# First chunk of a fused state space, retention and expert layer: B and C spread by matmuls, constants on three queues, weights centred earlier, own places for the end chunks

## What is computed

```python
x = _layernorm(x + mamba(x, ...))            # state space part, 256 channels, 16 states
x = _layernorm(x + retention(x, ctx, ...))   # 64 x 64 scores per sequence, decay mask
x = _layernorm(x + experts(x, ...))          # 16 experts, top 2, and a shared one

# mamba
x_b, z = jnp.split(x @ W_in, 2, axis=-1)
xc = _silu(conv_b + sum(xpad[:, k:k + T, :] * conv_w[:, k] for k in range(4)))
proj = xc @ W_xproj                          # 8 + 16 + 16 columns
delta_raw, B_in, C_in = ...                  # the three parts of proj
delta = jax.nn.softplus(delta_raw @ W_dt + b_dt)
A_bar = jnp.exp(delta[..., None] * -jnp.exp(A_log))
Bx = delta[..., None] * B_in[:, :, None, :] * xc[..., None]
# h = A_bar * h + Bx along the tokens; y = sum over states of h * C_in, + D_param * xc
out = (y * _silu(z)) @ W_out
```

## Time and profile before

| what | value |
|---|---|
| median of 3 runs | 1140.01 us (1138.7 to 1140.21) |
| the profiled execution | 1139.9 us, of which its span is 1138.0 us |
| mean granted clock of TensorE | 0.976 |
| DVE busy | 1047.7 us (92%) |
| PE, ACT, POOL busy | 1036.2, 992.5, 991.4 us |
| first drive starts | 30.17 us |
| last scan starts | 1062.91 us |

### The profile page before, as it was taken

One profiled execution on the slowest core, in us unless ns is written; L12 is line 12 of the kernel. 1 busy time (PEld: TensorE's weight loads), 2 busy tenths in 40 slices (PEclk: granted clock), 3 DMA queues, 4 the chain that ended last, 5 costly groups with the idle time before them and its releaser, 6 DMA issues. The chain is left out here.

```text
span 1138.0 us, 18240 instructions
## 1 busy us (share of the span) xinstructions
PE 1036.2 (91%) x5831; PEld 738.1 (65%) x5831; DVE 1047.7 (92%) x1458; ACT 992.5 (87%) x2159; POOL 991.4 (87%) x608
## 2 busy tenths in 40 slices
PE   5686888999999999999999999999999999989997
PEld 3464666676766766676676767667676767666665
DVE  2999999999999999999999999999999999999521
ACT  5878799999999999998989999899999999898442
POOL 0577798999989898998989899898989999899854
PEclk9778899999999999999999999999999999999999
DMA  6544454555546464555646455564736556453221
GB/s 159 204 162 159 160 176 162 179 191 180 189 167 200 166 196 177 186 179 177 206 148 218 148 187 182 177 201 156 228 136 213 193 178 194 169 185 116 84 94 52
DMA packets 84111, 194.49 MB, mean 171 GB/s; under 512 B 17288, under 2 KB 47936, under 8 KB 67632
## 3 DMA queue, kind: packets, MB, share of 16 engines
q1 hardware_dynamic: 84016, 193.33, 51.0%
HBM read 179.14 MB, written 5.77 MB: 162 GB/s over the span
## 5 line engine op out<-in xcount | busy, mean ns | idle before, releaser
L937 POOL TENSOR_TENSOR read<-state,bc_all 128x1024 f32<-128x1024 f32 x256 | 605.2, 2368 | 53.7 <-DVE state L811 43.9
L811 DVE TENSOR_TENSOR_SCAN state<-decay,drive_bank 128x512 f32<-128x512 f32 (+1 forms) x464 | 594.4, 1316 | 3.6 <-POOL read L937 1.9
L761 ACT ACTIVATE decay<-delta,a_neg 128x252 f32<-128x252 f32 x1024 | 422.5, 495 | 0.9
L803 DVE TENSOR_TENSOR drive_bank<-dx_bank,bc_all 128x512 f32<-128x512 f32 (+1 forms) x496 | 330.1, 702 | 0.3 <-DMA bc_all<-bc_dram 0.2
L373 PEld LDWEIGHTS y_bank<-ident,read 128*128 128x128 f32 x2048 | 241.0, 145 | 87.3 <-POOL read L937 46.4
L373 PE MATMUL y_bank<-ident,read 128*128 128x128 f32 x2048 | 277.4, 280 | 21.2 <-POOL read L937 20.9
L982 POOL TENSOR_TENSOR hid<-gu,comb_all 128x512 f32<-128x512 f32 (+1 forms) x136 | 165.3, 1216 | 21.3 <-DVE gu L897 12.4
L364 PEld LDWEIGHTS down_bank<-down_w,hid 128*128 128x128 f32 x1024 | 127.1, 192 | 30.7 <-issue 27.5
L731 ACT ACTIVATE silu<-bank 128x512 f32<-128x512 f32 (+1 forms) x153 | 87.6, 575 | 58.9 <-PE bank L364 58.2
L364 PE MATMUL down_bank<-down_w,hid 128*128 128x128 f32 x1024 | 136.0, 277 | 1.5 <-POOL hid L982 1.5
L364 PE MATMUL bank<-x2T,up_w 128*128 128x512 f32 (+1 forms) x272 | 132.1, 570 | 0.7 <-ACT silu L731 0.7
(11 more groups left out here) (127 smaller groups left out, 1358.7 us busy)
## 6 DMA issues: line engine op xcount, KB each, us to landing
bc_all<-bc_dram SPq DMA_DIRECT2D x128, 1024.0 KB, 4.9
comb_all<-comb_dram SPq DMA_DIRECT2D x240, 128.0 KB, 4.8
x_in<-in_x_dram SPq DMA_DIRECT2D x15, 256.0 KB, 5.3
ctx_in<-in_ctx_dram SPq DMA_DIRECT2D x15, 256.0 KB, 5.3
k_pair<-k_pair SPq DMA_DIRECT2D x30, 128.0 KB, 2.4
q_pair<-q_pair SPq DMA_DIRECT2D x30, 128.0 KB, 2.1
out_dram<-y_out SPq DMA_DIRECT2D x15, 256.0 KB, 6.1
comb_all<-comb_dram SPq DMA_DIRECT2D x32, 64.0 KB, 2.6
```

Of the source, the lines that this page charges most:

```text
L761: done = e.activation(seqs(decay_t[j % DECAYS][:, i, h, :])[:, :, 1:T], seqs(delta[c % 2][:, h, sub * SUB:(sub + 1) * SUB])[:, :, 1:T], AC ...
L803: e.tensor_tensor(drive_bank[:, a:b, :, :], dx_bank[:, :, :].unsqueeze(1).to_broadcast(shape), bc_all[group % BC_BUFS][:, 0, PAIR * i + a: ...
L811: e.tensor_tensor_scan(states(state_t[j % STATE_BUFS], a, b), states(decay_t[j % DECAYS], a, b), states(drive_bank, a, b), 0.0, ALU.mult, ...
L937: e.tensor_tensor(read_t[j % READS][:, :, :, :], state_t[j % STATE_BUFS][:, :, :, :], bc_all[group % BC_BUFS][:, 1, PAIR * i:PAIR * (i + 1 ...
```

## The change

1. **B and C of the first group by matmul.** For chunk 0 PE multiplies a column of the identity, spread over 128 output columns, with the 40 rows of `proj`; each product is one row of `proj` on all 128 partitions. Eight of them (256 columns each) fill `down_bank` and `y_bank`, two at a time, as scratch; DVE copies them to `bc_all` in four instructions (128x512). Groups 1 and on of chunk 0 still go through `bc_dram`.
2. **Chunk 0's short path.** DVE, not ACT, copies `proj`; DVE writes `dx_bank` directly, with neither POOL's `dx` nor ACT's copy. `d_diag` moves to just before the first drive. `w_dt` is loaded and used with 8 rows, not padded to 40 with zeros.
3. **Constants on three queues.** ACT issues `ident`, `a_log`, `conv_w`, and the two of `conv_b`; POOL issues `w_out` and `down_w` behind its memsets; SP the rest, where `qkv_rows`, `router_rows`, `shared_rows` come at tick -15, and the others at ticks -7 and 1, behind the store of chunk 0's B and C. The shared semaphores are split by what they cover.
4. **Tables.** ACT runs a one-column activation with Exp at the start, with Silu after the first `xT` and with Softplus after the first `xc`, so that the table of each is loaded there. `a_neg` is made by ACT at the start.
5. **Centring.** `w_out` and `down_w` are centred right after chunk 0's third tap, before the copy of `proj`; `w_qkv` and `shared_w` after the fourth scan. Chunk 1's three taps move behind the first drive and scan.
6. **Places.** `AT` gets five columns (all chunks, last, last but one, first, second). The last but one is the old common column. The common one differs from the old in some places, by up to 15 ticks.

```diff
+COLUMN = [3, 4] + [0] * (CHUNKS - 4) + [2, 1]
...
-    "y_gated": [(41, 56), (69, -24)],
+    "y_gated": [(40, 56, 41, -2, 38), (69, -24, 69, 36, 68)],
...
-    "comb_load": [(136, 134), (143, 149), (144, 156), (150, 169), (154, 181), (157, 190), (159, 212), (166, 235)],
+    "comb_load": [
+        (140, 134, 140, 102, 136), (143, 149, 143, 112, 137), (147, 156, 144, 119, 140), (151, 169, 150, 127, 142),
+        (152, 181, 154, 137, 162), (154, 190, 157, 138, 163), (169, 212, 159, 146, 166), (174, 235, 169, 151, 167)],
...
# PE
-                        mm(bank.t[:, 0:width(c)], w_dt[:, h * P:(h + 1) * P], proj[:, 0:width(c)]).then_inc(S["dt_mm"], 1)
+                        mm(bank.t[:, 0:width(c)], w_dt[:, h * P:(h + 1) * P], proj[0:DT_RANK, 0:width(c)]).then_inc(S["dt_mm"], 1)
                         bank.free = (S["delta"], at(c, h, 2))
+                    if c == 0:
+                        for two in (0, 1):
+                            for pair in (0, 1):
+                                w.wait_ge(S["bc_copy"], 2 * two + pair - 1)
+                                for i in range(PAIR):
+                                    row = DT_RANK + GROUP * pair + PAIR * two + i
+                                    done = mm((down_bank, y_flat)[pair][:, i * SUB:(i + 1) * SUB],
+                                              ident[0:PROJ, row:row + 1].to_broadcast([PROJ, P]), proj[0:PROJ, 0:SUB])
+                                done.then_inc(S["bc_mm"], 1)
...
# ACT
+            def warm(i, func):
+
+                e.activation(warmed[:, i:i + 1], eps_col[:, 0:1], func, scale=1.0)
...
+            e.dma_start(ident[:, :], io["c_ident"]).then_inc(S["ident"], 16)
+            e.dma_start(a_log[:, :, :], io["L0_attn_A_log"].rearrange("(h p) n -> p h n", p=P)).then_inc(S["a_log"], 16)
+            e.dma_start(conv_w[:, :, :], io["L0_attn_conv_w"].rearrange("(h p) k -> p h k", p=P)).then_inc(S["conv_consts"], 16)
+            per_channel(e, conv_b, io["L0_attn_conv_b"], S["conv_consts"])
+            w.wait_ge(S["zero"], DECAYS + 2)
+            warm(0, ACT.Exp)
+            w.wait_ge(S["a_log"], 16)
+            e.activation(a_exp[:, :, :], a_log[:, :, :], ACT.Exp, scale=1.0).then_inc(S["a_exp"], 1)
+            w.wait_ge(S["a_exp"], 1)
+            e.activation(a_neg[:, :, :], a_exp[:, :, :], ACT.Copy, scale=-1.0).then_inc(S["a_neg"], 1)
...
# DVE
+            def bc_copy(two, pair):
+
+                w.wait_ge(S["bc_mm"], 2 * two + pair + 1)
+                e.tensor_scalar(bc_all[0][:, pair, PAIR * two:PAIR * (two + 1), :].rearrange("p n t -> p (n t)"),
+                                (down_bank[:, :], y_flat)[pair], 1.0, 1.0, ALU.mult, ALU.mult).then_inc(S["bc_copy"], 1)
...
+                    w.wait_ge(S["proj_mm"], 1)
+                    e.tensor_scalar(proj[:, 0:SUB], bank_of["proj", 0][0:PROJ, 0:SUB], 1.0, 1.0, ALU.mult, ALU.mult).then_inc(
+                        S["proj"], 1)
...
+                    bc_copy(0, 0)
+                    w.wait_ge(S["delta"], 2)
+                    w.wait_ge(S["xc"], HALVES)
+                    e.tensor_tensor(dx_bank[:, :, :], xc[0][:, :, 0:SUB], delta[0][:, :, 0:SUB],
+                                    ALU.mult).then_inc(S["first_dx"], 1)
+                    bc_copy(0, 1)
+                    bc_copy(1, 0)
+                    bc_copy(1, 1)
+                    w.wait_ge(S["d_consts"], 16 * 2)
...
-                        (0, -3, ((w_out[:, :, :], 0, HALVES), (down_w[:, :, :], HALVES, PAIRS))),
-                        (1, 5, ((w_qkv[:, 2:3, :], HALVES + PAIRS, 1), (shared_w[:, 2:3, :], HALVES + PAIRS + 1, 1)))):
+                        (0, CENTER_TICK, ((w_out[:, :, :], 0, HALVES), (down_w[:, :, :], HALVES, PAIRS))),
+                        (1, 15, ((w_qkv[:, 2:3, :], HALVES + PAIRS, 1), (shared_w[:, 2:3, :], HALVES + PAIRS + 1, 1)))):
...
# POOL
+            e.dma_start(w_out[:, :, :], io["L0_attn_W_out"].rearrange("(h p) n -> p h n", p=P)).then_inc(S["out_consts"], 16)
+            e.dma_start(down_w[:, :, :], io["L0_ffn_down_proj"].rearrange("k e d -> (k e) d").rearrange(
+                "(j p) d -> p j d", p=P)).then_inc(S["out_consts"], 16)
```

More of the change, by code:

```diff
@@ L289, in blocks_of, with loads @@
             return width(c) // P
+        def loads(buffer, groups):
+            return uses(groups, buffer, BC_BUFS) - (1 if buffer == 0 else 0)
         def uses(before, buffer, buffers):
@@ L788, in _ @@
                     for h in range(HALVES):
-                        e.tensor_scalar(d_diag[:, h, :], ident[:, :], d_param[:, h:h + 1], 1.0, ALU.mult, ALU.mult)
-                    w.wait_ge(S["a_exp"], 1)
-                    e.tensor_scalar(a_neg[:, :, :], a_exp[:, :, :], -1.0, 1.0, ALU.mult, ALU.mult).then_inc(
-                        S["mamba_dve"], 1)
+                        done = e.tensor_scalar(d_diag[:, h, :], ident[:, :], d_param[:, h:h + 1], 1.0, ALU.mult, ALU.mult)
+                    done.then_inc(S["d_diag"], 1)
@@ L1029, in _ @@
-            e.dma_start(gate_w[:, :, :], io["L0_ffn_gate_proj"].rearrange("k d e -> d k e")).then_inc(late, 16)
-            e.dma_start(up_w[:, :, :], io["L0_ffn_up_proj"].rearrange("k d e -> d k e")).then_inc(late, 16)
-            for i in range(2):
-                e.dma_start(ctx_t[i][:, 0:blocks_of(i), :], rows_of(io["ctx_1024"], i)).then_inc(S[f"ctx_load{i}"], 16)
-            for tick in range(FIRST_TICK, LAST_TICK):
+            e.dma_start(w_dt[:, :], io["L0_attn_W_dt"]).then_inc(early, 16)
```

313 lines of the change are left out of this document (170 added, 143 removed), and 5 rows, old and new, of the table EXP_AT.

## The result

The changed kernel took 1144.65 us in the median of 9 runs (1140.29 to 1151.66), the kernel before 1140.01; the ratio is 1.0048, with a 95% interval of 1.0024 to 1.0071. It is 0.5% slower, where 0.7% faster was forecast. A second set of 12 runs of the same code gave 1.0051 (1.0031 to 1.0072). Two things stand out beside the median: the spread of its runs is 11 us, that of nine runs of the kernel before under 4; and the profiled execution, 1140.29 us with a span of 1138.5, is the fastest of the nine. What it shows is the loss of a good execution.

A forecast was written before the change was run, and what follows sets the result against it. DVE, with hardly a gap, was taken to bound the body of 256 steps, between a head and a tail chain. 1139.9 - 5.8 (head) - 2.4 (body waits) - 0.3 (tail) = 1131.4, said as 1131.5; range 1127.5 to 1137.0 us.

The forecast's parts named there:

- The head: Start until the first drive: from 30.17 to 22.3 us, less 2.1 for chunk 1's taps, a gain of 5.8 us.
- The 3.0 us taken for the landing of the tap rows: Head: SP's third transfer, issued by 1.7, lands in 3.0 us; `w_tap` is done by 5.8, no obstacle.
- a rise inside the new matmuls: Head, PE: TensorE's clock rises during the new matmuls, between 4.1 and 7.1 us for them; first drive at 22.3.
- Rival B: Head: `w_out` and `down_w` come late on POOL's queue and delay the copy of `proj`; landing at 13: 1135. Chance 0.08.
- Rival D: Head: something else sets the first drive, ACT's start or late B and C groups; 2 us left, 1138. Chance 0.08.
- Rival A: Head, PE: clock stays low through all new matmuls; first drive 24.3, head gain 3.8, 1133.4 us. Chance 0.18.
- The taps: Chunk 1's three taps, 2.27 us of DVE, move from before the first drive into the body; 2.1 us taken.
- DVE's busy time was to rise by 3 to 4 us: Sign of being right: DVE's busy time rises by the copies, 3 to 4 us, all in the head.
- The passage on the queues: Head: by the skill's rule, spreading constants over queues is worth only the issues' time, 0.50 us each, 2.5 us.
- `w_qkv`'s centring stays in the body either way: Head sum: this centring is in the body before and after the change, so it was given no cost.
- They can take away only waits: Body: the changed common places remove only DVE waits, 2.4 us of 5.3 taken off, bounds 0 and 5.3.
- Rival C: Body, common chunks: DVE's scans wait for POOL's `read`; with 1.0 us in each of 13, 1144.5. Chance 0.10.

The follow-up runs named there:

- again: The changed kernel run once more, for a second trace, against the kernel before: 1144.59 us, ratio 1.0051.
- part_c15: Changed kernel with only the retention and expert operations of chunks 0 and 1 at the old kernel's places: 1137.22 us, ratio 0.9984 to the kernel before.
- c01_part: Changed kernel, `w_qkv` and `shared_w` centred after the fourth step's drives, chunks 0 and 1's retention and expert operations at old places: 1134.89 us, 0.9953 to the kernel before.
- c1_common: Changed kernel, `w_qkv` and `shared_w` centred after the fourth step's drives, chunk 1's retention and expert operations at common places: 1151.47 us, 1.0091 to the kernel before.
- headfill: Changed kernel, `w_qkv` and `shared_w` centred after the fourth step's drives, seven matmuls of zeros in PE's idle time before 12 us: 1141.82 us, 1.0011 to the kernel before.

## Why the prediction was wrong

**Right, in part by luck.** The head came out near its forecast times: `xT` ended at 5.35 (5.5 forecast), `w_xproj` ran 12.43 to 13.49 (11.0 to 12.9 forecast), the centring 10.46 to 13.80, the first decays began at 17.13, ahead of the drive, and the first drive at 21.45 and 22.24 (22.3). The 3.0 us taken for the landing of the tap rows were 5.3 in fact, and the quicker matmuls made up for it. That was luck, and so was the time of the new matmuls: I had `w_xproj` and `w_dt` at the lower level and a rise inside the new matmuls. In the traces of the changed kernel and of `again` TensorE is at its upper level from `w_xproj` on and falls inside them (from 1.02 us for four recorded ones to 2.07 and 1.91), and no trace here has the rise. Rival B was not seen: `row_sum` never waited for POOL's transfers. Rival D neither. Rival A is real, in some executions, worth 4 us in the head. The taps cost 1.9 us against 2.1.

DVE's busy time was to rise by 3 to 4 us and rose by 8.5 (1047.7 to 1056.2): 3.6 are the copies, `dx_bank` and `proj`, 2.7 the centring below, 1.5 the 32 multiplies by the gate, whose move the forecast had at nothing. The passage on the queues put item 3 at the time of its issues, 2.5 us for the five that ACT has. It did not weigh that the store of B and C had stood 5.1 us in SP's queue (17.00 to 22.14) and no longer would.

**Wrong, first step: "`w_qkv`'s centring stays in the body either way".** I costed a moved step at nothing since its work is the same. Its work is; its neighbours are not. Beside a `read` that has just begun this instruction waits for nearly all of it. That term was 0 and is 2.7 us in the trace, 3 to 3.5 in the time. A row that could have told is in DVE's timeline of before; POOL's `read` stands below it:

```profile
35.77 0.40 DVE L841 TENSOR_SCALAR row_mean<-row_sum 128x2 f32<-128x2 f32 x1
33.78 2.37 POOL L937 TENSOR_TENSOR read<-state,bc_all 128x1024 f32<-128x1024 f32 x1 [12.82 <-DVE state L811]
```

The same operation on ten columns took 0.17. It ended at 36.17, POOL's `read` at 36.15; I took no notice of 0.2 us.

**Wrong, second step: "They can take away only waits".** I weighed the new common places and took 2.4 us off. Measured alone they move the median by nothing that can be measured (0.9997, 0.9988 to 1.0006), though the gaps in their trace fell from 5.40 to 2.54. The places of chunks 0 and 1, which the forecast didn't cost at all, were another matter. Those of their retention and expert operations were the loss, 7.5 us in the time (in the traces 5 us of gaps, 9.08 against 4.11 in `part_c15`). As I read it, this is the ramp, where the expert part of chunk 0 meets the retention of chunk 1 and the lists of three engines are new to each other; no run shows that this meeting is the cause. Rival C had the right kind of mechanism, but I put it into the common chunks, on POOL, and the waits were in the first four, mostly on PE and ACT.

The forecast's sum with the terms as measured: 1139.9 - 8.7 + 1.9 + 2.7 (centring) + 3.7 (gaps) + 1.3 (drives and scans, a term that I didn't have) = 1140.8 at the 128th scan; 0.7 us more came up to the last scan, and the tail was 1.1 us shorter, so 1140.4, where the profiled execution took 1140.3. The median is 4 us above that. What makes the spread is open. The level of TensorE in the head can be a part (4 us between the first drives of traces of the same start), but with the head filled the spread was still 8 us. It is 3 us in six runs with the places and the centring undone, so waits in the ramp may multiply it; that is not shown. No execution of 1151 us of the changed kernel was caught by the profiler.

Open: which of the 47 operations of the retention and expert part is the badly placed one. `c01_part` moves them together. That `c1_common` made it 8 us worse shows only that chunks 0 and 1 have to be placed with each other.

## What to carry to other kernels

Where the bound engine has hardly a gap behind its start, a quicker start is worth about as much at the end (a delay of 4 us put in by hand came out as 3.5; in `c01_part` the first drive is 8.1 us sooner, 1.9 go for the taps, and 5.3 come out), but only if the order behind it still fits: where a hand-written order is changed in many places at once, give each group of places its own run. Read the small instructions of the bound engine for length, not only its gaps: two of them held 2.7 us that no list of waits names. And before a trip through memory is replaced by matmuls, look for what its store waits for: of the thirteen microseconds from `proj` to the first drive here, five were a place in a queue.

## What the runs showed of the hardware

A DVE instruction can be held while a GpSimd instruction runs, and its recorded length grows by the wait: `row_mean` of two columns took 0.17 us with POOL idle, and 0.40, 0.86 and 2.05 us beside POOL's `read`, each time ending within 0.05 us of it. In `c01_part` a router instruction of 128x32 did the same beside POOL's `k_pair` (120.14 to 122.48); in the kernel before the same instruction took 0.19 us:

```profile
121.09 1.45 DVE L952 TENSOR_TENSOR above<-logits,top 128x32 f32<-128x32 f32 x1
122.46 0.15 DVE L954 TENSOR_TENSOR lead<-top 128x2 f32<-128x2 f32 x1
```

Others were not held beside a `read`: `row_sum` (0.27), and the drives and scans, which have an operand in PSUM (0.69 and 1.21). The Trainium skill has the rule, in "SBUF — State Buffer" (section "Who interferes with whom"): DVE shares one pair of its ports with GpSimd, and needs it in its mode with two ports, which operations like that of `row_mean` can enter; whichever is issued first keeps the pair for its whole instruction while the other is blocked. The same section has an instruction with two SBUF inputs contend with a GpSimd instruction that reads SBUF, and `tensor_reduce` never contend on trn2. The lengths above agree with all three: `row_mean` held, the subtraction of `w_qkv` from two SBUF operands 1.32 us beside `dx` and 0.29 alone, `row_sum` free. The forecast should have weighed this rule at the centring and didn't; by it the new place, just behind a scan, where POOL's `read` of the same state has just begun, is nearly the worst in a step.

With the same code up to there PE's `w_xproj` instructions took 1.06 us in one execution and 1.93 in another. So the code of the head alone does not decide TensorE's level there. Filling PE's idle time from 1 us on (`headfill`) gave the upper level for the tap products already (1.96 us for eight, against 3.32 in the changed kernel), and yet the last two of the new matmuls' groups ran at the lower one (2.00 and 1.91 us).
